# Another order of work in the attention loop of an adaLN, FFT-attention and MoE kernel

## The chip, the cores and the metric

The kernel runs on one core of a Trainium2 chip. The metric is the device time of one execution in microseconds (us), lower is better; the times shown are medians of several executions.

## The reference

Input x is 4 sequences of 1024 tokens with 256 channels, 4096 tokens in all. Cut to what matters:

```python
mod = (silu(c) @ wmod).reshape(4, 6, 1, 256)          # sa, ca, ga, sb, cb, gb; ga, gb kept at least 0.25 from 0
h = layernorm(x) * (1 + ca) + sa
q, k, v = (unit(h @ W.T + b) for each of Wq, Wk, Wv)  # unit(a) = ifft(fft(a) / (|fft(a)| + 1e-8)).real
s = cumsum(bind(k, v), axis=1)                        # bind: product of spectra
x = x + ga * unbind(s, q)                             # unbind: product with the conjugate spectrum
h = layernorm(x) * (1 + cb) + sb
x = x + gb * moe(h)                                   # 8 experts, top 2 of h @ gate_w, swiglu, 256 -> 512 -> 256
```

## The kernel before, in words

The program has three stages: the attention loop (to about 255 us), the routing (to about 300 us) and the expert stage (to the end). The change touches the first and its tail.

The projections and the FFT are one matrix product: `transform_weights` multiplies each of Wk, Wv, Wq with the DFT matrix, so that a projection gives the spectrum at once, with real and imaginary parts of 128 frequencies on the partitions and 512 tokens in a row. The 129th (Nyquist) frequency goes by narrow matmuls of its own (L490, L494). The tokens are worked in 8 blocks of 512 (`NBLK`, t = 0 to 7), two to a sequence. A block passes these steps, engine by engine:

- ScalarE makes the normalized rows (`normal_rows`, L801, with the standard deviation from `project`, L793, and VectorE's `ln1_moments` L1106, L1109 and `ln1_rows` L1117, L1119). TensorE transposes them (L462), ScalarE brings them to SBUF as `h_t` (`spectra`, L815), TensorE multiplies (L484, 24 matmuls, six PSUM banks "z").
- ScalarE evacuates the six banks (`evacuate`, L830), squares them (L840) and the Nyquist columns (L837, L838). VectorE adds the squares (`magnitudes`, L1180), ScalarE takes `roots` (L850).
- VectorE's `bind` (L1132 to L1167) divides by the magnitudes (a reciprocal, L1140), multiplies key and value spectra and sums along the tokens with two scans (L1164, L1167). GpSimd multiplies with the query (L1544, four operations), and on even t scales the inverse DFT for a sequence right behind (L1553, two operations). VectorE's `unbind` (L1174, L1175) adds up, `nyquist_sums`, `nyquist_apply` (L503, L504, L1125) and `nyquist_row` (L560, L946) do the same for the Nyquist row.
- TensorE's `inverse` (L576, L580) goes back to rows of tokens. ScalarE copies them (`residual`, L870), a GpSimd DMA adds x (L1539), VectorE takes moments (`residual`, L1188) and normalizes (`ln2_rows`, L1314, L1319), ScalarE and GpSimd split into two fp16 halves (`split_rows` L881, `low_rows` L1530), TensorE transposes them (`gate_rows`, L515), ScalarE copies (L857), TensorE multiplies by the gate matrix (`gate`, L527), ScalarE copies the gates (L862), and VectorE picks the best two experts (`top2`, L1197, L1201).

Beside this, the expert weights are prepared: SP loads chunks of 512 KB (`load_weights`, L337), ScalarE rounds them to fp16 (`split_weights`, L887), TensorE makes the remainder (`low_piece`, L540, L541; four pieces i = 0 to 3 per block, two chunks), and ScalarE stores it (L894), which frees the stage for the next load.

Every engine has its own queue with a loop written by hand, t from -1 to 7. Iteration t works on several blocks at once: the projection of block t + 1, bind, unbind and inverse of block t, the second normalization of block t - 1, and the gates of block t - 2. The order within an iteration is the order of the calls; the engines meet at semaphores only. The four PSUM banks 4 to 7 go round (`rot`) in an order that `psum_plan` writes out: an item takes the bank of the item four places before it, and TensorE waits (`bank_free`) until that one has been read.

At the start VectorE makes the modulation rows (`modulation`), SP stores them as a small table, broadcasts it and only then loads weight chunks 2 and on. At the end VectorE goes on with `early_picks` for blocks 0 to 5, and the last block runs in halves.

## Time and profile before

| | |
|---|---|
| median of 3 runs | 638.22 us (636.01 to 638.6) |
| the profiled execution, its own time | 634.83 us |
| its span, first to last instruction | 633.0 us |
| mean granted clock of TensorE in it | 0.935 |
| TensorE busy with matmuls | 565.5 us |
| VectorE busy | 490.1 us |
| ScalarE busy | 301.8 us |
| GpSimd busy | 322.2 us |

In the profile PE is TensorE, PEld its weight loads, DVE VectorE, ACT ScalarE, POOL GpSimd and SP SyncE. L484 is line 484 of the kernel. A row of a timeline gives start, duration, engine, line, operation, output from input, how many instructions are merged, and in brackets how long the engine was idle before and what ended the wait. A row of the view by windows gives the window, its length, the busy time of PE, PEld, DVE, ACT and POOL with their instructions, the granted clock of TensorE (1.00 is full), the busy share of the DMA engines and GB/s.

### The profile page before, as it was taken

The page shows a single profiled execution, that of the slowest core. Times are in us where ns is not written, and L with a number is a line of the kernel's source. Part 1 is how long each engine was busy: PE and PEld are TensorE (multiplying, and loading weights), DVE is VectorE, ACT ScalarE, POOL GpSimd, SP SyncE. Part 2 cuts the span into 40 slices and gives each one's busy share as a digit, 9 for nine tenths or more (in the row PEclk, how much of TensorE's full clock was granted, in tenths as well). Part 3 has the DMA queues.
Part 4 walks back from the last instruction along what each step waited for, and adds up shares of the span by engine and source line. Part 5 has one row for each costly group of instructions (what it writes and reads, how often), then busy time and mean ns, then how long its engine had stood idle before and what let it go on. Part 6 is the DMA issues. An engine that isn't in the chain of part 4 may idle for free.

```text
span 633.0 us, 13199 instructions
## 1 busy us (share of the span) xinstructions
PE 565.5 (89%) x4005; PEld 428.1 (68%) x4006; DVE 490.1 (77%) x1058; ACT 301.8 (48%) x497; POOL 322.2 (51%) x213
## 2 busy tenths in 40 slices
PE   6888999899999966559699999999999999999982
PEld 5444554555546543326488888888888888888871
DVE  1238789989998988897378888888888888888881
ACT  3664877877786762532333333333333333333330
POOL 0002132441413243000638888888888888888554
PEclk9798999989997995857799999999999999999996
DMA  9213273652735328622747777777777777777632
GB/s 318 86 61 124 67 204 100 193 149 83 216 101 169 102 88 285 211 38 67 196 62 134 135 138 135 137 136 134 134 135 133 133 133 133 133 134 134 98 35 34
DMA packets 86942, 82.93 MB, mean 131 GB/s; under 512 B 48628, under 2 KB 76276, under 8 KB 86648
## 3 DMA queue, kind: packets, MB, share of 16 engines
q0 software_dynamic: 18480, 34.51, 30.3%
q1 hardware_dynamic: 67128, 47.07, 25.9%
q10 hardware_dynamic: 1296, 0.87, 0.4%
q8 instruction: 21, 0.34, 0.2%
q14 instruction: 17, 0.14, 0.1%
HBM read 45.90 MB, written 23.15 MB: 109 GB/s over the span
## 4 chain that ended last, share of the span: by engine, by line
PE 70%; DVE 12%; ACT 6%; issue 6%; DMA 3%; POOL 1%; POOLq 0%; SPq 0%; ACTq 0%; DVEq 0%
PE ps L703 33%; PE ps L720 16%; PE ps L484 9%; PE ps L540 3%; ACT region L801 2%; PE ps L494 2%; PE ps L636 1%; DMA w_stage<-in_w 1%; ACT region L857 1%; DVE region L1140 1%; DVE region L1180 1%; PE ps L425 1%; POOL region L1544 1%; PE ps L527 1%; DMA region<-in_dft 1%
## 5 line engine op out<-in xcount | busy, mean ns | idle before, releaser
L703 PE MATMUL ps<-region,w_sb 128*128 128x256 f16 x1872 | 213.4, 275 | 2.7 <-ACT region L939 2.7
L703 PEld LDWEIGHTS ps<-region,w_sb 128*128 x1872 | 184.2, 99 | 25.7 <-issue 3.0
L1574 POOL DMA_INDIRECT out_rows<-w_stage,region x78 | 150.5, 1930 | 48.5 <-DVE w_stage L1491 26.5
L1564 POOL DMA_INDIRECT region<-h_scratch,region x78 | 106.0, 1359 | 71.4 <-DVE region L1437 47.9
L1459 DVE TENSOR_SCALAR region<-ps,region 128x256 f32<-128x256 f32 x156 | 68.1, 478 | 61.0 <-PE ps L703 60.9
L720 PE MATMUL ps<-region 128*128 x936 | 110.2, 275 | 3.4 <-DVE region L1473 3.4
L720 PEld LDWEIGHTS ps<-region 128*128 128x128 f16 x936 | 92.3, 99 | 15.0 <-issue 3.6
L1015 ACT ACTIVATE region<-ps,region 128x256 f32<-128x256 f32 x156 | 65.5, 471 | 76.4 <-PE ps L703 76.4
L1025 ACT ACTIVATE region<-region 128x1024 f16<-128x1024 f32 x39 | 41.2, 1058 | 125.3 <-DVE region L1467 125.3
L484 PE MATMUL ps<-region 128*128 128x512 f32 x192 | 88.3, 617 | 8.4 <-ACT region L815 6.0
L1544 POOL TENSOR_TENSOR region<-region 128x512 f32<-128x512 f32 x32 | 39.7, 1267 | 94.3 <-DVE region L1167 94.3
L484 PEld LDWEIGHTS ps<-region 128*128 128x128 f32 x192 | 37.1, 198 | 55.1 <-issue 47.3
L1467 DVE SCALAR_TENSOR_TENSOR region<-region 128x1024 f32<-128x1024 f32 x39 | 47.8, 1225 | 1.4
L1473 DVE SCALAR_TENSOR_TENSOR region<-region 128x1024 f16<-128x1024 f32 x39 | 47.5, 1219 | 1.1 <-ACT region L1025 1.1
L540 PE MATMUL ps<-w_stage,ident_sw 128*128 128x512 f32 x72 | 43.7, 692 | 0.0
L1530 POOL TENSOR_TENSOR region<-region 128x1024 f16<-128x1024 f32 x6 | 12.8, 2129 | 59.7 <-ACT region L881 52.4
L830 ACT ACTIVATE region<-ps,region 128x512 f32<-128x512 f32 x48 | 32.1, 684 | 12.8 <-PE ps L484 12.6
L1491 DVE SCALAR_TENSOR_TENSOR w_stage<-w_stage,region 128x256 f32<-128x256 f32 x78 | 34.0, 477 | 0.0
L1485 DVE SCALAR_TENSOR_TENSOR w_stage<-ps,region 128x256 f32<-128x256 f32 x78 | 29.1, 414 | 4.5 <-PE ps L720 4.5
L894 ACT ACTIVATE w_sb<-ps 128x512 f16<-128x512 f32 x32 | 19.2, 599 | 16.9 <-PE ps L541 16.5
L1140 DVE RECIPROCAL region<-region 128x516 f32<-128x516 f32 x8 | 27.0, 3378 | 0.3
L1464 DVE TENSOR_SCALAR region<-region 128x1024 f32<-128x1024 f32 x39 | 26.6, 683 | 0.0
(208 smaller groups left out, 683.8 us busy)
## 6 DMA issues: line engine op xcount, KB each, us to landing
w_stage<-in_w SPq DMA_DIRECT2D x20, 512.0 KB, 3.6
region<-in_x SPq DMA_DIRECT2D x8, 512.0 KB, 8.2
out_rows<-region SPq DMA_DIRECT2D x8, 512.0 KB, 3.0
h_scratch<-gb_bc SPq DMA_DIRECT2D x4, 1024.0 KB, 6.8
h_scratch<-region SPq DMA_DIRECT2D x8, 512.0 KB, 3.0
region<-region POOLq DMA_DIRECT2D x7, 512.0 KB, 4.6
region<-in_ramp SPq DMA_DIRECT2D x1, 2064.0 KB, 10.8
region<-in_w SPq DMA_DIRECT2D x4, 512.0 KB, 5.1
```

The lines of the kernel that those rows point to most:

```text
L484: mm = pe.matmul(rot(("z", t, i)), w_spec[:, c, k, r * P:(r + 1) * P], h_t[:, k, :], start=(k == 0), stop=(k == KD - 1))
L540: pe.matmul(rot(("lo", t, i)), ident_sw[:], staged(n)[:, at:at + BLK], start=True, stop=False)
L703: mm = pe.matmul(ps[:, GV + 2 * half + a, (f % 2) * MT:(f % 2 + 1) * MT], w, xg_t[:, s, xa * KD + k, :], start=(n == 0), stop=(n == 3 * KD ...
L720: mm = pe.matmul(ps[:, YB + s, u * D:(u + 1) * D], hid[:, s, xa, k, u * P:(u + 1) * P], w, start=(n == 0), stop=(n == 3 * KF - 1))
L1015: ins = nc.scalar.activation(gs[:, 2 * half + f, :], ps[:, 4 + 2 * half, f * MT:(f + 1) * MT], ACT.Gelu_apprx_sigmoid, scale=1.0 / SUP, bi ...
L1025: nc.scalar.activation(hid[:, s, HI], vv[:, s], ACT.Copy, scale=SH / SUP).then_inc(hid_hi, 1)
L1459: ins = V.tensor_scalar(vv[:, s, 2 * half + f, :], ps[:, 5 + 2 * half, f * MT:(f + 1) * MT], b1_t[:, bass.ds(e, 1), 1, 2 * half + f], (LIM ...
L1467: V.scalar_tensor_tensor(out=vv[:, s], in0=vv[:, s], scalar=(1.0 - LIMIT) * SUP, in1=gs, op0=ALU.max, op1=ALU.mult).then_inc(h_ready, 1)
L1473: V.scalar_tensor_tensor(out=hid[:, s, LO], in0=vv[:, s], scalar=SH / SUP, in1=hid[:, s, HI], op0=ALU.mult, op1=ALU.subtract).then_inc(hid ...
L1544: ins = G.tensor_tensor(prod[:, a, r, 0:BLK], s_run[:, s, a, :], z[:, s, QRY, r, 0:BLK], ALU.mult)
L1564: G.indirect_dma_start(out=xg_rows[:, t % XG, u, :], out_offset=None, in_=h_scratch, in_offset=bass.IndirectOffsetOnAxis(ap=gather_idx[:, ...
L1574: G.indirect_dma_start(out=out, out_offset=bass.IndirectOffsetOnAxis(ap=scatter_idx[:, at:at + 1], axis=0), in_=y_sb[:, t % 2, u, :], in_o ...
```

## The change

The work stays the same; its order changes, on all of TensorE, ScalarE and VectorE.

- TensorE: the projection is cut into `project` (transposes), `transform` and `nyquist_cols`. Low piece 0 of a block goes between the last two, low piece 1 ahead of `nyquist_sums`. At t = -1 the transposes of block 1 and low piece 0 come behind the modulation rows. The PSUM plan follows.
- ScalarE: low piece 0 is stored ahead of the third square. The Nyquist columns are copied behind that square, and count `ny_out` twice. Gate rows come ahead of the two standard deviations, these ahead of low piece 1. Normal rows come ahead of low piece 3, and the roots behind it. At the start the roots of block 0 stand between the first two weight splits, the spectra of block 1 follow the modulation copies, and splits 2 and 3 move behind the last bank of block 1.
- VectorE: `top2` works on block t - 3 in place of t - 2 and stands ahead of `nyquist_apply`; `ln1_rows` goes ahead of `unbind`; `modulation` goes into bind(0), behind its second operation, and `magnitudes(0)` no longer waits for it. `top2(5)` comes behind the loop, ahead of `early_picks`.

```diff
--- before.py
+++ after.py
@@
     items = []
     for t in range(-1, NBLK + 2):
         if t + 1 < NBLK:
-            items += [("z", t + 1, i) for i in range(6)] + [("ny", t + 1, 0)]
+            items += [("z", t + 1, i) for i in range(6)]
+        if t == -1:
+            items += [("ny", 0, 0), ("lo", 0, 0)]
+        elif t < NBLK:
+            items.append(("lo", t + 1, 0))
+            if t + 1 < NBLK:
+                items.append(("ny", t + 1, 0))
+        if t < NBLK:
+            items.append(("lo", t + 1, 1))
         if 0 <= t < NBLK:
             items.append(("pre", t, 0))
-        if t < NBLK:
-            items.append(("lo", t + 1, 0))
         if t >= 2:
             items.append(("gate", t - 2, 0))
         if t < NBLK:
-            items += [("lo", t + 1, 1), ("lo", t + 1, 2)]
+            items.append(("lo", t + 1, 2))
         if 0 <= t < NBLK:
             items.append(("row", t, 0))
         if t < NBLK:
@@
             n = place[item] - ROT
             if n >= 0:
                 kind, t, i = order[n]
-                s, v = {"z": (z_ready, 6 * t + i + 1), "ny": (ny_out, t + 1), "pre": (ny_done, t + 1),
+                s, v = {"z": (z_ready, 6 * t + i + 1), "ny": (ny_out, 2 * t + 2), "pre": (ny_done, t + 1),
                         "lo": (w_lo[i % 4 // 2], 2 * t + i % 2 + 1),
                         "gate": (gate_ready, t + 1), "row": (row_ready, t + 1)}[kind]
                 e.wait_ge(s, v)
@@
                 if t >= 4:
                     pe.wait_ge(h2t_ready, KD * (t - 3))
                 transpose_rows(n_sb, t, tp_done)
+
+            def transform(t):
+
                 for i in range(6):
                     c, r = i // 2, i % 2
                     bank_free(pe, ("z", t, i))
@@
                         mm = pe.matmul(rot(("z", t, i)), w_spec[:, c, k, r * P:(r + 1) * P], h_t[:, k, :],
                                        start=(k == 0), stop=(k == KD - 1))
                     mm.then_inc(z_mm, 1)
+
+            def nyquist_cols(t):
+
                 bank_free(pe, ("ny", t, 0))
                 if t == 0:
                     pe.wait_ge(const_in, 48)
@@
 
             transform_weights()
             for t in range(-1, NBLK):
-                if t + 1 < NBLK:
-                    project(t + 1)
                 if t == -1:
+                    project(0)
+                    transform(0)
+                    nyquist_cols(0)
                     modulation_rows()
+                    project(1)
+                    low_piece(0, 0)
+                elif t + 1 < NBLK:
+                    if t >= 1:
+                        project(t + 1)
+                    transform(t + 1)
+                    low_piece(t + 1, 0)
+                    nyquist_cols(t + 1)
+                else:
+                    low_piece(t + 1, 0)
                 if t >= 2:
                     gate_rows(t - 2)
-                if 0 <= t < NBLK:
+                low_piece(t + 1, 1)
+                if t >= 0:
                     nyquist_sums(t)
-                low_piece(t + 1, 0)
                 if t >= 2:
                     gate(t - 2)
-                low_piece(t + 1, 1)
                 low_piece(t + 1, 2)
                 if t >= 0:
                     nyquist_row(t)
@@
                         act.wait_ge(z_mm, 6 * t + 2 * c + r + 1)
                         nc.scalar.activation(z[:, t % 2, c, r, 0:BLK], rot(("z", t, 2 * c + r)), ACT.Identity,
                                              bias=bias_f[:, 3 * r + c:3 * r + c + 1]).then_inc(z_ready, 1)
-                    if c == 2:
-                        act.wait_ge(nymm, t + 1)
-                        if t < 2:
-                            act.wait_ge(ny_zero, t + 1)
-                        cols = rot(("ny", t, 0))[:, 0:3 * TPB].rearrange("p (j c) -> p c j", j=TPB)
-                        nc.scalar.activation(mag[:, t % 2, :, BLK:NB], cols, ACT.Square)
-                        nc.scalar.activation(z[:, t % 2, :, RE, BLK:NB], cols, ACT.Copy).then_inc(ny_out, 1)
+                    if c == 2 and t == 1:
+                        split_weights(2)
+                        split_weights(3)
+                    if c == 2 and t >= 1:
+                        low_piece(t, 0)
                     act.wait_ge(z_ready, 6 * t + 2 * c + 2)
                     nc.scalar.activation(sq[:, c], z[:, t % 2, c, :, 0:BLK], ACT.Square).then_inc(sq_ready, 1)
                     if c == 0 and t >= 2:
                         residual(t - 2)
+                act.wait_ge(nymm, t + 1)
+                if t < 2:
+                    act.wait_ge(ny_zero, t + 1)
+                cols = rot(("ny", t, 0))[:, 0:3 * TPB].rearrange("p (j c) -> p c j", j=TPB)
+                nc.scalar.activation(mag[:, t % 2, :, BLK:NB], cols, ACT.Square).then_inc(ny_out, 1)
+                nc.scalar.activation(z[:, t % 2, :, RE, BLK:NB], cols, ACT.Copy).then_inc(ny_out, 1)
 
             def std2(t):
                 act.wait_ge(ln2_agg, TPB * (t + 1))
@@
 
             def roots(t):
                 act.wait_ge(mag_ready, t + 1)
+                act.wait_ge(ny_out, 2 * t + 2)
                 nc.scalar.activation(mag[:, t % 2], mag[:, t % 2], ACT.Sqrt).then_inc(root_ready, 1)
 
             def gate_rows(t):
@@
                     evacuate(t + 1)
                 if t == LAST:
                     residual(t - 1)
+                    low_piece(NBLK, 0)
+                if t == -1:
+                    split_weights(0)
+                    roots(0)
+                    split_weights(1)
+                    modulation_rows()
+                    spectra(1)
+                    low_piece(0, 0)
                 if t >= 2:
                     gate_rows(t - 2)
-                if t == -1:
-                    split_weights(0)
-                    split_weights(1)
-                    modulation_rows()
-                low_piece(t + 1, 0)
+                if t >= 0 and t + 2 < NBLK:
+                    project(t + 2)
+                if t >= 1:
+                    std2(t - 1)
+                low_piece(t + 1, 1)
                 if t >= 2:
                     gate(t - 2)
-                if t >= 1:
-                    std2(t - 1)
-                if t >= 0 and t + 2 < NBLK:
-                    project(t + 2)
-                low_piece(t + 1, 1)
                 low_piece(t + 1, 2)
                 if t >= 0:
                     nyquist_row(t)
+                if t >= 0 and t + 2 < NBLK:
+                    normal_rows(t + 2)
                 low_piece(t + 1, 3)
-                if t + 1 < NBLK:
+                if 0 <= t < NBLK - 1:
                     roots(t + 1)
                 if t >= 0 and t + 2 < NBLK:
-                    normal_rows(t + 2)
-                if t + 2 < NBLK:
                     spectra(t + 2)
-                if 1 <= t <= NBLK:
+                if t >= 1:
                     split_rows(t - 1)
-                split_weights(2 * t + 4)
-                split_weights(2 * t + 5)
+                if t >= 0:
+                    split_weights(2 * t + 4)
+                    split_weights(2 * t + 5)
 
             last_residual(0)
             last_std(0)
@@
                 dve.wait_ge(eps_ready, t + 1)
                 V.scalar_tensor_tensor(out=den, in0=mag[:, s, KEY, :], scalar=EPS_UNIT, in1=mag[:, s, VAL, :],
                                        op0=ALU.add, op1=ALU.mult).then_inc(den_ready, 1)
+                if t == 0:
+                    modulation()
                 dve.wait_ge(den_ready, t + 1)
                 V.scalar_tensor_tensor(out=rec, in0=mag[:, s, QRY, :], scalar=EPS_UNIT, in1=den,
                                        op0=ALU.add, op1=ALU.mult).then_inc(all_ready, 1)
@@
                     residual(t - 1)
                 if t >= 0 and t + 2 < NBLK:
                     ln1_moments(t + 2)
+                if t >= 3:
+                    top2(t - 3)
                 if 0 <= t < NBLK:
                     nyquist_apply(t)
-                    if t >= 2:
-                        top2(t - 2)
+                    if t + 2 < NBLK:
+                        ln1_rows(t + 2)
                     unbind(t)
                     if t + 1 < NBLK:
                         magnitudes(t + 1)
                 if t == -1:
                     ln1_rows(1)
-                    modulation()
                     magnitudes(0)
-                if t >= 0 and t + 2 < NBLK:
-                    ln1_rows(t + 2)
                 if t >= 1:
                     if t == 1:
                         dve.wait_ge(mod_in, 16)
                     ln2_rows(t - 1)
 
+            top2(LAST - 2)
             early_picks()
             low_rows(LAST - 1)
             for h in range(2):
```

## Rows read from the trace of the kernel before

**Rows 1.** By windows: blocks 2 to 6, expert stage; busy time, clock.

```profile
96.41:232.06 135.65, 127.31 (x630) 75.21 (x630) 124.17 (x271) 102.48 (x156) 44.85 (x36) 0.95 0.47 136
300.00:633.00 333.00, 313.37 (x2827) 277.59 (x2825) 253.93 (x509) 111.80 (x201) 255.88 (x156) 0.97 0.67 123
```

**Rows 2.** What VectorE waited for, 96 to 232 us: total, times, longest.

```profile
DVE best L1197 <- ACT gates L862: 9.4, 5, 2.6
```

**Rows 3.** Timeline of VectorE, block 3 of the loop: start, duration, instruction, idle before.

```profile
122.85 0.42 DVE L1132 TENSOR_SCALAR region<-region 128x516 f32<-128x516 f32 x1
...
135.79 1.26 DVE L1167 TENSOR_TENSOR_SCAN region<-region 128x512 f32<-128x512 f32 x1
...
140.39 0.13 DVE L1125 TENSOR_TENSOR region<-ps,region 128x4 f32<-128x4 f32 x1
142.73 0.37 DVE L1197 MAX8 best<-gates 128x8 f32<-128x8 f32 x4 [2.21 <-ACT gates L862]
...
143.70 0.67 DVE L1174 TENSOR_TENSOR region<-region 128x512 f32<-128x512 f32 x1
...
150.08 0.42 DVE L1132 TENSOR_SCALAR region<-region 128x516 f32<-128x516 f32 x1
```

**Rows 4.** Timeline of VectorE, block 7: last scan and unbind.

```profile
245.01 1.26 DVE L1167 TENSOR_TENSOR_SCAN region<-region 128x512 f32<-128x512 f32 x1
...
251.41 0.69 DVE L1174 TENSOR_TENSOR region<-region 128x512 f32<-128x512 f32 x1 [2.17 <-POOL region L1544]
```

**Rows 5.** Timeline of GpSimd and VectorE where they meet, blocks 0 and 4.

```profile
64.58 1.69 POOL L1553 TENSOR_TENSOR region<-region 128x256 f32<-128x256 f32 x2
...
154.48 2.14 POOL L1530 TENSOR_TENSOR region<-region 128x1024 f16<-128x1024 f32 x1 [12.31 <-ACT region L881]
...
65.69 1.12 DVE L1175 TENSOR_TENSOR region<-region 128x512 f32<-128x512 f32 x1
...
155.41 1.76 DVE L1142 SCALAR_TENSOR_TENSOR region<-region 128x516 f32<-128x516 f32 x1
```

**Rows 6.** Timeline of ScalarE and VectorE at the start of the loop.

```profile
33.25 0.69 ACT L830 ACTIVATE region<-ps,region 128x512 f32<-128x512 f32 x1 [1.03 <-PE ps L484]
...
43.96 1.48 ACT L850 ACTIVATE region<-region 128x1548 f32<-128x1548 f32 x1
...
52.92 1.06 ACT L887 ACTIVATE w_sb<-w_stage 128x1024 f16<-128x1024 f32 x1 [6.13 <-DMA w_stage<-in_w]
...
39.61 0.40 DVE L1092 TENSOR_SCALAR region<-region 4x512 f32<-4x512 f32 x1 [18.67 <-issue]
...
42.11 1.74 DVE L1180 TENSOR_TENSOR region<-region 128x1536 f32<-128x1536 f32 x1
45.48 0.43 DVE L1132 TENSOR_SCALAR region<-region 128x516 f32<-128x516 f32 x1 [1.63 <-ACT region L850]
```

**Rows 7.** Timeline of ScalarE behind unbind, block 3.

```profile
146.24 0.57 ACT L946 ACTIVATE region<-ps 1x512 f32<-1x512 f32 x1
147.26 0.60 ACT L894 ACTIVATE w_sb<-ps 128x512 f16<-128x512 f32 x1 [0.45 <-PE ps L541]
147.75 1.49 ACT L850 ACTIVATE region<-region 128x1548 f32<-128x1548 f32 x1
149.14 2.06 ACT L801 ACTIVATE region<-region 128x256 f32<-128x256 f32 x4
```

**Rows 8.** TensorE, block 3; same work in blocks 3, 5, 6, windows.

```profile
124.57 10.54 PE L484 MATMUL ps<-region 128*128 128x512 f32 x24 [0.53 <-ACT region L815]
...
135.36 1.95 PE L494 MATMUL ps<-region 128*128 128x3 f32 x16
...
137.17:144.47 7.30, 7.30 (x52) 4.56 (x52) 4.99 (x31) 4.19 (x9) 4.96 (x4) 0.53 0.57 181
192.07:199.23 7.16, 7.16 (x51) 4.47 (x50) 4.71 (x31) 4.19 (x9) 4.88 (x4) 0.52 0.66 220
220.22:225.25 5.03, 4.40 (x52) 2.86 (x52) 2.26 (x18) 3.90 (x8) 5.03 (x5) 1.00 0.41 139
```

## The prediction

> **What bounds the kernel now.** I read the stages first (the view by windows), then what VectorE waits for, then one block of the attention loop on each engine, and last the start and the end of the loop. Blocks are counted by t, and a block begins here where VectorE begins bind(t) (L1132).
>
> The five blocks from bind(2) at 96.41 to bind(7) at 232.06 take 135.65 us, 27.13 each. VectorE is busy for 124.17 of them and TensorE for 127.31 [rows 1]. The expert stage from 300 us on is none of the change's lines, with TensorE busy for 313.37 of 333.00; I carry it over unchanged. VectorE's idle time in the five blocks has one cause: top2 waits for the gates that ScalarE copies, 9.4 us in five waits [rows 2]. TensorE is nearly as full, so taking the wait away helps only as far as TensorE, ScalarE and GpSimd keep up.
>
> Block 3 [rows 3]: bind starts at 122.85, its last scan ends at 135.79 + 1.26 = 137.05, so bind is 14.2; the moments go on to 140.39. Top2 can start only at 142.73 and takes 0.97. From unbind's start, 143.70, to bind(4), 150.08, are 6.4: unbind twice 0.6, then magnitudes, ln1_rows (some 0.3) and ln2_rows. In block 7 top2 hardly waits, and what unbind then waits for is GpSimd: the scan ends at 246.27, unbind starts at 251.41, 5.14 later [rows 4]. That is the floor behind the present wait.
>
> **The change, part by part.**
>
> *Top2 a block later, ln1_rows ahead of unbind.* No instruction goes. The gates are then a block old and wait for nothing. Between the scan and unbind VectorE has in block 3 the moments (3.4), nyquist_apply (0.13), top2 (0.97) and ln1_rows (0.3), together 4.8, less than GpSimd's 5.14: the GpSimd floor sets unbind. An odd block becomes 14.2 + 5.14 + 6.4 - 0.3 = 25.4, where 6.4 - 0.3 is 1.2 of unbind and 4.9 behind it.
>
> *Collisions with GpSimd.* In even blocks GpSimd goes on at once with L1553. At t = 0, where unbind too had waited for GpSimd, L1553 starts at 64.58, and unbind's second operation takes 1.12 and ends at 66.81, 2.2 behind that start, against 1.2 in block 3 [rows 3, 5]. Even blocks will meet this each time: I take 2.1. On the other side, at t = 4 the low rows (GpSimd from 154.48) meet L1142, which takes 1.76 [rows 5]. With ScalarE earlier the low rows fall under the reciprocal, so I take 14.0 for an even bind, a little under the 14.2 of block 3; at 14.2 the sum would be 0.6 later. An even block becomes 14.0 + 5.14 + 2.1 + 4.9 = 26.15. The Trainium skill, SBUF — State Buffer, section "SBUF: two separate sides", says that the port pair which VectorE and GpSimd share is an exclusive lock and that the loser blocks for the whole instruction. The trace nearly agrees: the low rows end at 154.48 + 2.14 = 156.62, and L1142, begun at 155.41, ends 0.55 behind that [rows 5]. By the rule in full, with unbind behind both halves of L1553, an even block would by my estimate be up to 0.7 longer, and the forecast some 2.5 us later.
>
> *Five blocks.* Three even and two odd ones: 3 x 26.15 + 2 x 25.4 = 129.3 against 135.65, so 6.35 less, if nothing else comes late.
>
> *ScalarE's order behind unbind.* Today it is nyquist_row 0.57, low piece 0.60, roots 1.49, then normal_rows 2.06 [rows 7]. After: nyquist_row, normal_rows, low piece, roots. As they overlap, 0.6 + 2.0 + 0.5 + 1.5 + 0.1 to see it = 4.7 behind unbind, against VectorE's own 4.9 (magnitudes and ln2_rows). The later roots cost nothing in steady blocks, by 0.2 us only. In block 0 there are no ln2_rows to cover them, and they end 1.3 later than they could; that is in the start below. In exchange normal_rows no longer stand between the roots and the transposes, and TensorE, which waited at that place, goes on straight from inverse.
>
> *Low piece 0 and the Nyquist columns.* TensorE does the same work. ScalarE's third square comes a low-piece copy later, but the magnitudes that need it are several us away. Splitting ny_out costs nothing. Pushing project (ln1's std) ahead of gate and low piece 1 makes these wait for ln1's moments, 3.4 behind the scan; ScalarE leaves the gate rows at about that moment, and behind it wait low piece 1, gate, low piece 2 and the row's bank: 0 to 0.5, hidden, since nyquist_row waits for unbind anyway. The weight loads on SP wait for low piece 3, now some 1.7 later; the load's landing comes shortly ahead of its split, and a late one is covered by ScalarE's slack ahead of the fifth projection bank.
>
> *TensorE's room.* It is busy 25.5 a block, with clock drops in it. In block 3 the granted clock is 0.53 for a stretch right behind the narrow Nyquist matmuls, nearly all of it at the lower level, 1.2 GHz; gate rows to low piece 1 take 7.30 there. In block 5 the same work takes 7.16, and in block 6, at full clock, 4.40 of busy time [rows 8]: 2.9 more for each drop. Without the two, (127.31 - 5.8) / 5 = 24.3, plus 0.5 for the wait for ScalarE's spectra [rows 8], the one that stays: 24.9 against the new 25.8. So it fits, and where a drop comes it does not: of 2.9 I count 1.2 as delay of the next bind (the row then comes 1.4 later, less the 0.2 above). Two drops: 2.4.
>
> *The start.* Today ScalarE evacuates the last bank of block 0 at 33.25 [rows 6], and behind its third square come two weight splits, the modulation copies and low pieces, and the roots only at 43.96, because VectorE makes the modulation rows (39.61 to 42.11) ahead of the magnitudes; bind(0) starts at 45.48 [rows 6]. After: square from 33.9, magnitudes 35.1 to 36.8, roots to 38.3, bind(0) at 38.4. Its first two operations end at 39.6; the modulation waits for ScalarE's copies (roots, one split, then copies: 40.5) and takes 2.6, to 43.1; the rest of bind is 14.0 - 1.2 = 12.8, so the scans end at 55.9, against 45.48 + 14.0 = 59.5. SP waits for the modulation's last operation before it stores the table, broadcasts it and loads weights; that comes 0.9 later. Today ScalarE waits 6.13 for the first of those chunks, to 52.92, ahead of evacuating block 1 [rows 6]; after the change they land at 53.9 and about 55, and ScalarE reaches them at 55.3, behind the last bank of block 1 (TensorE starts that transform at 44.2 behind the low pieces, and it takes 10.5). TensorE then waits for these splits to about 56.4, low piece and Nyquist columns to 59.8, low piece 1 and sums to 61.3; unbind(0) starts at 61.8, ends at 63.7, and nyquist_row to roots takes 4.7: bind(1) at 68.4. Then an odd block, 25.4: bind(2) at 93.9 against 96.41. Gain 2.5, less 0.5 if TensorE's clock drops over its 1.9 us wait (I leave it to the range).
>
> *The end.* Bind(7) on is as today: unbind waits for GpSimd anyway. Top2(4) fills that wait, and top2(5), 0.97, goes ahead of the early picks; VectorE comes to wait for the last residual there, so 0 to 1. Low pieces 0 and 1 leave the path ahead of the last inverse, up to 0.5 gained; if TensorE's clock is low there, up to 1.5 is lost. I take 0.
>
> **Sum.** 2.5 + 6.35 - 2.4 = 6.5 us. The profiled execution took 634.83 (span 633.0), so 628.3 for it. It is 3.4 below the median of the runs shown, 638.22; the same gain from the median is 631.7.
>
> **Rivals.**
> 1. *TensorE sets the pace.* Its order gives it work packed denser, but it is near full, and a clock drop in each block instead of two in five costs three more times 1.2 to 1.5, with something similar in block 1. Gain 2.0: 636.2. For it: 25.5 busy a block. Against: without drops it has 0.9 of room.
> 2. *The roots take the place of the gates.* They have 0.2 us of cover. If ScalarE's row copy is 0.9 later than reckoned, each of seven blocks loses 0.7: 4.9 lost, gain 1.6: 636.6. For it: at 45.48 bind was released by the roots, after 1.63 of waiting [rows 6]. Against: in block 3 the roots end at 149.24, 0.8 before bind(4) [rows 3, 7], and the new order takes 0.6 of it.
> 3. *The slower side: half clock over the projection.* The projection's 24 matmuls take 10.54 at full clock [rows 8]. A stretch of 7 us at half clock, like that of block 3, adds 3.5 there; TensorE's room is 0.9, so 2.6 a block reach VectorE. Three such blocks eat 7.8 and level the gain; all five of the loop give 13, that is 13 - 8.85 = 4.1 slower: 642.3. It decides from the fourth block on. For it: TensorE will stand still ahead of inverse and, in block 0, for the weight splits. Against: the two drops shown came behind the narrow Nyquist matmuls [rows 8], and the change puts full-width work on both sides of them.
> 4. *It does nothing:* the order moves but other waits of the same length come up; 638.
>
> **Chances.** Forecast 0.66; rival 1 0.13, rival 2 0.08, rival 3 0.07, rival 4 0.06. The range runs from 627.0 (no clock drop, 2.4 more, and some on the start and end; 638.22 - 8.85 is 629.4, less the spread of the runs) to 637.0, which takes in rivals 1 and 2. Half a percent, 3.2 us, is what a measurement of this kernel can tell from no change: faster means below 635.0. Faster: most of the forecast and a part of rivals 1 and 2, 0.75; same 0.17; slower 0.08.
>
> **What would show it.** VectorE: no wait at L1197 ahead of the tail; unbind released by GpSimd's multiplications 5.14 behind the scan; even unbinds near 2.1, L1142 at 0.70; blocks of 25.4 and 26.2. bind(0) near 38.4, bind(2) near 93.9, bind(7) near 223 to 226. ScalarE: no 6 us wait for weights at the start. The forecast is wrong if bind waits for roots in many blocks (rival 2), if TensorE's low clock shows in more than half the blocks (rivals 1 and 3), or if the stage from 300 us changes its length.

## The result and the profile after

The changed kernel takes 634.71 us (median of 18 executions, 631.34 to 640.01), the kernel before, on the same chip, 638.64 (18, 636.01 to 641.98). The ratio is 0.9943, 95% interval 0.9920 to 0.9965: faster by 0.57%, 3.9 us between the medians. The forecast was 631.7, a gain of 6.5. The profiled execution took 633.45 (span 631.6) against 634.83 (633.0): only 1.4 us less. That pair alone would mislead, and where the other 5 us of it are is half of what follows. The 634.83 is also none of the 18 executions of before above, and lies below all of them (636.01 to 641.98).

The loop first. The view by windows, with the stretches that answer to [rows 1]:

```profile
95.84:225.29 129.45, 124.97 (x620) 74.15 (x619) 124.89 (x260) 102.11 (x155) 44.86 (x36) 0.95 0.50 143
300.00:631.00 331.00, 314.21 (x2816) 278.00 (x2816) 252.43 (x507) 107.54 (x196) 250.03 (x151) 0.97 0.65 120
```

Five blocks take 129.45 instead of 135.65, and VectorE is busy for 124.89 of them. What it waited for from 96 to 226, 2.4 us in all, which answers to [rows 2]:

```profile
DVE region L1156 <- PE ps L516: 1.5, 1, 1.5
DVE region L1207 <- POOL region L1577: 0.6, 1, 0.6
DVE region L1148 <- ACT region L815: 0.3, 1, 0.3
```

The 9.4 us for the gates are gone. VectorE's timeline, first the end of block 0 with the start of block 1, then block 2 (L1156 is nyquist_apply, L1207 and L1208 unbind, L1163 the start of bind, L1213 the magnitudes):

```profile
53.94 1.20 DVE L1200 TENSOR_TENSOR_SCAN region<-region 128x512 f32<-128x512 f32 x1
...
63.16 0.16 DVE L1156 TENSOR_TENSOR region<-ps,region 128x4 f32<-128x4 f32 x1 [6.30 <-PE ps L516]
...
63.52 0.69 DVE L1207 TENSOR_TENSOR region<-region 128x512 f32<-128x512 f32 x1
...
64.72 1.75 DVE L1213 TENSOR_TENSOR region<-region 128x1536 f32<-128x1536 f32 x1
70.34 0.43 DVE L1163 TENSOR_SCALAR region<-region 128x516 f32<-128x516 f32 x1 [3.87 <-ACT region L877]
...
115.02 1.12 DVE L1207 TENSOR_TENSOR region<-region 128x512 f32<-128x512 f32 x1
116.06 1.12 DVE L1208 TENSOR_TENSOR region<-region 128x512 f32<-128x512 f32 x1
...
122.01 0.42 DVE L1163 TENSOR_SCALAR region<-region 128x516 f32<-128x516 f32 x1
```

Block 0 loses: 6.30 for TensorE's sums, then 3.87 for the roots. What held them, on TensorE (L552, L553 a low piece, L506 the Nyquist columns, L515 and L516 the sums) and ScalarE (L823 normal_rows, L921 a low piece's copy, L877 the roots):

```profile
55.81 1.12 PE L552 MATMUL ps<-w_stage,ident_sw 128*128 128x512 f32 x2 [1.72 <-ACT w_sb L914]
...
57.40 2.73 PE L506 MATMUL ps<-region 128*128 128x3 f32 x16
59.99 2.05 PE L552 MATMUL ps<-w_stage,ident_sw 128*128 128x512 f32 x2
61.84 0.63 PE L553 MATMUL ps<-w_sb,ident_neg 128*128 128x512 f16 x1
...
62.55 0.57 PE L516 MATMUL ps<-region 128*128 128x4 f32 x2
```

TensorE's window there (columns as in [rows 1]; the granted clock is the third number from the end):

```profile
60.00:63.00 3.00, 3.00 (x9) 1.69 (x9) 0.00 (x0) 0.93 (x4) 1.44 (x3) 0.50 0.00 0
```

```profile
66.39 2.06 ACT L823 ACTIVATE region<-region 128x256 f32<-128x256 f32 x4
68.36 0.57 ACT L921 ACTIVATE w_sb<-ps 128x512 f16<-128x512 f32 x1
68.84 1.48 ACT L877 ACTIVATE region<-region 128x1548 f32<-128x1548 f32 x1
```

TensorE waits 1.72 for the weight splits, and within the Nyquist columns, which take 2.73 where [rows 8] has 1.95, its clock falls to the lower level (0.50): the next low piece takes 2.05 + 0.63 where one at full clock takes 1.02 + 0.38. So bind(2) starts at 95.84, only 0.57 earlier than in [rows 1], though bind(0) started at 37.90, 7.58 earlier than in [rows 6]. From there the loop gains to 6.77 at bind(7), and all of it lasts to the first gather (292.55 against 299.32). The rest of the loss is at the entry of the expert stage, on TensorE (L705 transposes a tile's rows, L725 is the up-projection):

```profile
299.91 7.34 PE L725 MATMUL ps<-region,w_sb 128*128 128x256 f16 x47 [1.30 <-ACT region L966]
...
309.63 0.55 PE L705 MATMUL ps<-ident_h,region 128*128 128x128 f16 x7 [1.19 <-issue]
312.05 8.19 PE L725 MATMUL ps<-region,w_sb 128*128 128x256 f16 x48 [1.87 <-ACT region L966]
...
322.70 5.40 PE L725 MATMUL ps<-region,w_sb 128*128 128x256 f16 x48
```

and in the chain of waits that ended last (start, length, what):

```profile
303.72 6.12 another core or an unknown queue
```

From the first up-projection to the third are 22.79 us; in the profile of before they were 17.75:

```profile
306.19 8.03 PE L703 MATMUL ps<-region,w_sb 128*128 128x256 f16 x48 [1.30 <-ACT region L939]
...
323.94 5.40 PE L703 MATMUL ps<-region,w_sb 128*128 128x256 f16 x48
```

Of the 6.77 us gained at the first gather 5.04 go there. Is that the change's doing?

### The profile page after: what moved, and what is told of

Read it like the earlier page. It is cut to its first block, busy times and chain, and to the rows that moved or that the text cites. A ratio compares the mean times of both kernels' runs of the same rounds, so it can differ in the third digit from the quotient of the medians.

```text
span 631.6 us, 13207 instructions
## 1 busy us (share of the span) xinstructions
PE 570.7 (90%) x4005; PEld 431.1 (68%) x4006; DVE 492.5 (78%) x1058; ACT 301.1 (48%) x497; POOL 321.2 (51%) x213
## 4 chain that ended last, share of the span: by engine, by line
PE 64%; DVE 25%; issue 5%; ACT 3%; POOL 1%; another core or an unknown queue 1%; DMA 1%; POOLq 0%; ACTq 0%; DVEq 0%
PE ps L725 32%; PE ps L742 16%; PE ps L493 5%; DVE region L1173 3%; PE ps L552 2%; DVE region L1137 2%; DVE region L1213 2%; DVE region L1352 2%; PE ps L648 1%; DVE region L1347 1%; DVE region L1188 1%; DVE region L1182 1%; DVE region L1197 1%; DVE region L1200 1%; PE ps L506 1%
## 5 line engine op out<-in xcount | busy, mean ns | idle before, releaser
L725 PE MATMUL ps<-region,w_sb 128*128 128x256 f16 x1872 | 215.7, 276 | 3.4 <-ACT region L966 3.2
L725 PEld LDWEIGHTS ps<-region,w_sb 128*128 x1872 | 185.4, 99 | 27.2 <-issue 3.6
L493 PE MATMUL ps<-region 128*128 128x512 f32 x192 | 86.2, 606 | 3.9 <-ACT region L837 3.9
L552 PE MATMUL ps<-w_stage,ident_sw 128*128 128x512 f32 x72 | 46.9, 739 | 2.9 <-ACT w_sb L914 1.7
L921 ACT ACTIVATE w_sb<-ps 128x512 f16<-128x512 f32 x32 | 18.8, 588 | 15.8 <-PE ps L553 15.5
## 6 DMA issues: line engine op xcount, KB each, us to landing
region<-in_ramp SPq DMA_DIRECT2D x1, 2064.0 KB, 11.3
```

Source lines behind the costliest of these rows:

```text
L493: mm = pe.matmul(rot(("z", t, i)), w_spec[:, c, k, r * P:(r + 1) * P], h_t[:, k, :], start=(k == 0), stop=(k == KD - 1))
L552: pe.matmul(rot(("lo", t, i)), ident_sw[:], staged(n)[:, at:at + BLK], start=True, stop=False)
L725: mm = pe.matmul(ps[:, GV + 2 * half + a, (f % 2) * MT:(f % 2 + 1) * MT], w, xg_t[:, s, xa * KD + k, :], start=(n == 0), stop=(n == 3 * KD ...
```

## Experiments

Twelve runs in four groups, each group on one chip: top2 alone, the loop's part, the start's part and block 0 eased; the changed kernel again, roots first and block 0 in the old order; before again and the loop's part again; the last three. Each ratio is to executions of the kernel before on that chip, whose medians in the four groups are 634.01, 639.37, 638.58 and 634.33, so the chips differ by up to 5.4 us, as much as the change is worth. Profiled moments are compared with [rows 1] and [rows 6].

**Top2 alone.** Before, with top2 moved and nothing else.

```diff
+                if t >= 3:
+                    top2(t - 3)
                 if 0 <= t < NBLK:
                     nyquist_apply(t)
-                    if t >= 2:
-                        top2(t - 2)
                     unbind(t)
...
+            top2(LAST - 2)
             early_picks()
```

> The kernel before with one part of the change: top2 one block later and ahead of nyquist_apply. Theory A (the wait for the gates was the whole of the loop's loss; the new orders on ScalarE and TensorE only keep it away): VectorE's wait for the gates goes, unbind is released by GpSimd in each block, bind(2) to bind(7) takes 129 to 131 us instead of 135.65, and the run is 5 to 6.5 us ahead at the first gather, 0.5 to 0.9% less in the time. Theory B (the order of ScalarE matters as much: with the gates still behind the std and the square roots, everything that ScalarE does behind them comes late and the roots or nyquist_row take the place of the gates): bind(2) to bind(7) takes 132 to 134 us and the gain is 2 to 3.5 us.

632.55 us against 634.01, ratio 0.9985 (0.9955 to 1.0016): nothing. The wait for the gates is gone, as theory A said, and the time has not changed: bind(7) starts at 232.04, where it was at 232.06. Odd blocks fell from 27.2 or 27.4 to 26.4, even ones rose from 27.5 or 27.1 to 28.3 and 28.0. Block 4 on VectorE (L1142 is a step of bind, L1174 unbind), then GpSimd (L1531, the low rows):

```profile
149.28 0.43 DVE L1132 TENSOR_SCALAR region<-region 128x516 f32<-128x516 f32 x1 [0.59 <-ACT region L850]
...
154.62 2.56 DVE L1142 SCALAR_TENSOR_TENSOR region<-region 128x516 f32<-128x516 f32 x1
...
170.32 1.11 DVE L1174 TENSOR_TENSOR region<-region 128x512 f32<-128x512 f32 x1 [0.74 <-POOL region L1545]
171.36 1.12 DVE L1175 TENSOR_TENSOR region<-region 128x512 f32<-128x512 f32 x1
```

```profile
154.49 2.13 POOL L1531 TENSOR_TENSOR region<-region 128x1024 f16<-128x1024 f32 x1 [12.30 <-ACT region L881]
```

The low rows start at 154.49; in [rows 5] they started at 154.48. ScalarE releases them, and its pace had not changed. VectorE, 0.8 us earlier, now meets them whole: L1142 takes 2.56 instead of 1.76 there and 0.70 where they don't meet. Unbind, earlier too, runs into L1553's pair. Followed through: unbind(3) starts at 142.22 instead of 143.70, 1.48 earlier. The roots, at the same time as before because ScalarE waits for TensorE's low pieces (1.59 at L894), take 0.59 of it at bind(4) (and 0.57 at bind(6)), the low rows take 0.80, and unbind(4) ends where it did. Theory B named ScalarE and the roots, and part of the loss is there; the larger part, the low rows, neither theory had.

**The loop's part alone.** The changed kernel with the old start: modulation ahead of magnitudes(0) again, and on ScalarE

```diff
                     split_weights(0)
-                    roots(0)
                     split_weights(1)
                     modulation_rows()
-                    spectra(1)
                     low_piece(0, 0)
...
-                if 0 <= t < NBLK - 1:
+                if t < NBLK - 1:
                     roots(t + 1)
```

> The changed kernel with the start as it was before: no modulation inside bind(0), roots(0), spectra(1), the splits and the projection of block 1 in the old places. Theory A (the start is worth next to nothing, as its gain is eaten by nyquist_apply(0) waiting for TensorE): bind(0) near 45.5, bind(2) within 1 us of 96.4, bind(2) to bind(7) 129.5 us, time within 0.15% of the changed kernel. Theory B (the start is worth 2 to 3 us, and only the profiled run hid it): 0.3 to 0.5% slower than the changed kernel.

628.52 us (6 executions), ratio 0.9901 (0.9869 to 0.9933); but the profiled one was the slowest (633.02), with bind(0) at 47.94 and bind(2) at 99.84, so it was run again. The theories compared it with the changed kernel, which is not in this group; its median and those of the start's part and of block 0 eased (628.85, 628.15, below) agree within the intervals.

> The loop's new order with the old start, once more, since the profiled execution of the first run was its slowest (633.0 against 626.8 to 629.6) and had TensorE's clock at 0.90 in the first 100 us. Theory A (the loop's part is 6 to 7 us): bind(0) near 45.5, bind(2) within 1 us of 96.4, bind(7) near 226; 0.9 to 1.1% faster than before, no worse than the changed kernel (0.9943 and 0.9930 of before). Theory B (the loop loses in blocks 0 and 1 what it gains later): bind(2) near 99 again, bind(7) near 230, 0.3 to 0.6% faster.

637.85 us against 638.58, ratio 0.9982 (0.9950 to 1.0013), on another chip. No single number fits this kernel. Its twelve executions go with TensorE's mean granted clock: 632.8 to 633.0 at 0.94, one 635.1 at 0.93, 637.8 to 638.3 at 0.924 or 0.925, 640.5 to 641.2 at 0.915; those of before in that group lie between 636.0 and 641.9 at 0.927 to 0.933. The profiled one, at 0.924, has blocks 3, 4 and 5 at 26.59, 27.47 and 26.03, where the changed kernel has 25.47, 26.16 and 25.48, and block 0 at 28.34. In block 4 TensorE's window (columns as in [rows 1]), its low piece, and VectorE's next bind:

```profile
166.00:172.00 6.00, 6.00 (x55) 4.32 (x55) 5.54 (x32) 3.59 (x9) 5.78 (x6) 0.62 0.86 258
```

```profile
167.55 2.02 PE L552 MATMUL ps<-w_stage,ident_sw 128*128 128x512 f32 x2
...
178.80 1.04 PE L468 MATMUL ps<-ident_sb,region 128*128 128x128 f32 x8
```

```profile
178.90 0.43 DVE L1155 TENSOR_SCALAR region<-region 128x516 f32<-128x516 f32 x1 [1.07 <-ACT region L872]
```

So the half clock that costs the changed kernel's profile nothing costs this one 1.3 in block 4. The profile is theory B's (bind(2) at 98.68, bind(7) at 231.09), the time below even that. Block 0, in the new order with the old start, is longer in both profiles of this kernel (26.42 and 28.34) than before (25.13). Theory A's 0.9 to 1.1% shows only in the first run; that the clock makes the difference is read from the times and this one profile, no run shows it by itself.

**The start's part alone.** Before, with roots(0), spectra(1), the transposes of block 1 and the modulation where the change puts them, and the splits 2 and 3 one square later than there; TensorE's and ScalarE's order from block 0 on as before.

```diff
                     split_weights(0)
+                    roots(0)
                     split_weights(1)
                     modulation_rows()
+                    spectra(1)
...
+                if t == 0:
+                    modulation()
                 dve.wait_ge(den_ready, t + 1)
```

> The kernel before with the start of the change alone. Theory A: bind(0) near 38, but nyquist_apply(0) waits some 6 us for TensorE's sums, so that bind(2) is at most 1 us earlier than 96.41, and the loop from there takes 135.7 us as before: 0 to 0.15% faster. Theory B (without the loop's new order in block 0, where the roots stand ahead of normal_rows, bind(1) comes 2 us earlier than in the changed kernel, and the start keeps its 2.5 us): bind(2) near 94, 0.3 to 0.4% faster.

628.85 us, ratio 0.9935 (0.9907 to 0.9964). Bind(1) starts at 67.01 and bind(2) at 92.78, 3.6 ahead of before: theory B, and more than it said. The blocks from bind(2) to bind(7) take 133.26 here, 2.4 less than before, which no theory had. TensorE waits for the splits here too, 1.78, and runs at the lower clock after it, but the sums of block 0 stand ahead of that wait (L506, L507), so unbind is released by GpSimd and only the roots are still waited for, 1.27:

```profile
56.08 0.36 PE L507 MATMUL ps<-region 128*128 128x4 f32 x2
58.22 2.07 PE L543 MATMUL ps<-w_stage,ident_sw 128*128 128x512 f32 x2 [1.78 <-ACT w_sb L896]
```

```profile
61.62 1.11 DVE L1188 TENSOR_TENSOR region<-region 128x512 f32<-128x512 f32 x1 [3.39 <-POOL region L1557]
...
67.01 0.43 DVE L1144 TENSOR_SCALAR region<-region 128x516 f32<-128x516 f32 x1 [1.27 <-ACT region L859]
```

**Block 0 eased.** The changed kernel with nyquist_sums(0) right behind transform(1), and roots(1) ahead of nyquist_row(0); the two are not told apart.

```diff
                     transform(t + 1)
+                    if t == 0:
+                        nyquist_sums(0)
                     low_piece(t + 1, 0)
...
                 low_piece(t + 1, 2)
+                if t == 0:
+                    roots(1)
                 if t >= 0:
                     nyquist_row(t)
```

> The changed kernel with block 0 eased: TensorE makes the Nyquist sums of block 0 between the transform of block 1 and low piece 0, so ahead of the weight splits it waits for, and ScalarE makes the roots of block 1 ahead of nyquist_row and normal_rows. Theory A (the start's predicted 2 us were lost to these two orders): nyquist_apply(0) no longer waits over 1 us for TensorE, unbind(0) starts near 61 instead of 63.5, bind(1) near 66 instead of 70.3, bind(2) near 92, the first gather 3 to 4 us earlier, 0.4 to 0.6% faster than the changed kernel. Theory B (TensorE's own work in blocks 0 and 1 sets the pace there, so what is gained at bind(1) is lost at the projection of block 2): bind(1) earlier by 3 us, but bind(2) by under 1, and no difference in the time.

628.15 us, ratio 0.9908 (0.9876 to 0.9941). Unbind(0) at 61.62 and bind(1) at 67.23, 3.1 earlier than in the changed kernel; bind(2) at 95.62, 0.2 earlier: theory B by these moments. The time can't be set beside the changed kernel's, which is not in this group. The new order puts two low pieces ahead of the sums in block 1 as well, and TensorE, which starts the next transform 5.2 us behind bind(1) (3.6 with the start alone) and falls to half clock again, ends them late:

```profile
88.71 0.16 DVE L1162 TENSOR_TENSOR region<-ps,region 128x4 f32<-128x4 f32 x1 [1.23 <-PE ps L518]
```

**The changed kernel again.**

> The changed kernel, not altered. It tells whether the loss at the entry of the expert stage (first gather 6.8 us earlier than before, but the third up-projection only 1.2 us earlier) belongs to the change or to one execution. Theory A (one execution's clock and stall): the second up-projection again near 309 to 310 us, as the first gather is at 292.5, and a span near 627 us if nothing else comes. Theory B (the change's shorter routing window brings the stall): second up-projection near 312, span 630 to 632 us again.

633.16 us against 639.37, ratio 0.9930 (0.9903 to 0.9956). The entry stall came back unchanged: first up-projection at 299.73, second at 311.71, third at 322.44. That seemed theory B, until before was profiled again (below).

**Roots first.** The changed kernel with one piece undone.

```diff
-                if t >= 0 and t + 2 < NBLK:
-                    normal_rows(t + 2)
                 low_piece(t + 1, 3)
                 if 0 <= t < NBLK - 1:
                     roots(t + 1)
+                if t >= 0 and t + 2 < NBLK:
+                    normal_rows(t + 2)
```

> The changed kernel with one piece undone: ScalarE makes the square roots of block t+1 ahead of normal_rows(t+2), as before. Theory A (normal_rows early is what keeps GpSimd's low rows under VectorE's reciprocal): in blocks 2, 4 and 6 the low rows start 3.3 to 5.2 us behind bind instead of 2.3 to 2.8, and where it is over 4, L1175 takes 1.7 to 2.6 us instead of 0.69 and the block 27 to 28.3 instead of 26.17; bind(2) to bind(7) takes 131 to 134 us; block 0 on the other hand becomes 2 us shorter, as bind(1) no longer waits for the roots. Together -2 to +2 us against the changed kernel. Theory B (the place of normal_rows does not matter with the gate copies ahead of the std): every block stays at 26.2 and 25.5, and the kernel is 2 us faster than the changed one through block 0 alone.

637.87 us, ratio 0.9978 (0.9959 to 0.9996), 4.7 us above the changed kernel of the same group. Theory A, with a bigger loss: bind(2) to bind(7) takes 134.74. The low rows start 3.6 us behind bind in blocks 2 and 3, 4.05 in 4 and 6, and 5.21 in 5; L1175 takes 0.98, 1.41 and 2.55 where the changed kernel has 0.69. Over the five blocks that is 3.9 of the 5.3 us lost (134.74 against 129.45); the rest goes with waits for TensorE's sums (3.8 us in four, against 1.5 in one). Block 5, VectorE then GpSimd:

```profile
180.71 2.55 DVE L1175 SCALAR_TENSOR_TENSOR region<-region 128x516 f32<-128x516 f32 x1
```

```profile
180.58 2.13 POOL L1563 TENSOR_TENSOR region<-region 128x1024 f16<-128x1024 f32 x1 [11.22 <-ACT region L908]
```

In the changed kernel the low rows start 2.27 to 2.82 behind bind and end inside the reciprocal, which takes the 3.38 it takes everywhere. Block 4, VectorE then GpSimd:

```profile
149.39 3.38 DVE L1173 RECIPROCAL region<-region 128x516 f32<-128x516 f32 x1
```

```profile
150.30 2.13 POOL L1563 TENSOR_TENSOR region<-region 128x1024 f16<-128x1024 f32 x1 [8.97 <-ACT region L908]
```

Seven of the fourteen profiles (before in both, top2 alone, the start alone in both, block 0 eased, this one) have the step behind the reciprocal lengthened by the low rows. It ends 0.54 to 0.56 us behind them each time, however early it had begun. Block 0 became 1.4 us shorter, not 2.

**Block 0 in the old order.** The changed kernel, but for t = 0 TensorE's and ScalarE's order of before, with the splits kept early and the bank plan to match.

```diff
+                elif t == 0:
+                    transform(1)
+                    nyquist_cols(1)
+                    nyquist_sums(0)
+                    low_piece(1, 0)
                 elif t + 1 < NBLK:
...
                     roots(t + 1)
+                if t == 0:
+                    normal_rows(2)
```

> The changed kernel with block 0 in the old order on TensorE (Nyquist columns and sums of block 0 ahead of low piece 0) and ScalarE (roots ahead of normal_rows), and the weight splits ahead of the last square; from block 1 on the new order. Theory A (the change's start and its loop are each worth their gain, but the new order costs 3 us in block 0): bind(0) near 38.5, TensorE waits under 1 us for the splits, bind(1) at 66.5 to 67.5, bind(2) at 92.5 to 93.5, bind(7) near 222 to 223, some 3 us earlier than the changed kernel and 9 to 10 earlier than before; time 1.2 to 1.5% below before. Theory B (TensorE is behind from block 0 on and its low pieces stand in block 1's way): bind(2) near 95.5 as in the run with block 0 eased, no gain over the changed kernel.

629.34 us, ratio 0.9872 (0.9845 to 0.9900), on the chip where the changed kernel had 0.9930. Theory A: bind(1) at 64.74, bind(2) at 90.23, bind(7) at 220.76, 11.3 earlier than before. The splits are ready when TensorE comes to them, and there is no wait and no clock drop (from the second run of this kernel, below):

```profile
55.39 0.36 PE L518 MATMUL ps<-region 128*128 128x4 f32 x2
55.61 1.10 PE L554 MATMUL ps<-w_stage,ident_sw 128*128 128x512 f32 x2
```

**Before again.**

> The kernel before, not altered, for a second profile of it. Its first profile has no stall at the entry of the expert stage: from the first up-projection at 306.19 to the second 9.9 us, where four runs of the new order (the changed kernel twice, roots first, block 0 in the old order) have 12.0 to 12.1. Theory A (the stall belongs to a chip or an execution, not to the order of the loop): this profile can show it too, second up-projection 12 us behind the first, with ScalarE and VectorE standing until the same moment; the span is then 636 to 637 us instead of 633. Theory B (the change brings it): 9.9 us again. A profile without the stall at a time of 635 or less tells only that the fast case was met again.

638.88 against 638.58, ratio 0.9997 (0.9975 to 1.0020). The profile (span 637.6) has the stall. TensorE, then ScalarE and VectorE, which both stand until 317.2:

```profile
307.16 7.85 PE L703 MATMUL ps<-region,w_sb 128*128 128x256 f16 x48 [1.30 <-ACT region L939]
...
316.93 0.27 PE L683 MATMUL ps<-ident_h,region 128*128 128x128 f16 x2 [1.15 <-issue]
319.27 6.93 PE L703 MATMUL ps<-region,w_sb 128*128 128x256 f16 x48 [2.07 <-ACT region L939]
...
328.66 5.40 PE L703 MATMUL ps<-region,w_sb 128*128 128x256 f16 x48
```

```profile
317.18 0.84 ACT L1015 ACTIVATE region<-ps,region 128x256 f32<-128x256 f32 x2 [6.21 <-remote]
```

```profile
317.17 1.66 DVE L1459 TENSOR_SCALAR region<-ps,region 128x256 f32<-128x256 f32 x4 [11.56 <-remote]
```

Theory A: the stall comes without the change too. The third up-projection comes at 328.66, 21.50 behind the first.

**The three on one chip.**

> The start's part alone, on one chip with the two runs that follow, since the parts have so far been timed on different chips. Theory A (each part is worth its gain, and the change loses some of the start's in block 0): bind(1) near 67, bind(7) near 226 to 227, 0.5 to 0.8% below before, the same as the changed kernel within the intervals. Theory B (the 0.65% of the first run was that chip's): 0 to 0.3% below before.

> The new order with block 0 in the old order, again. Theory A: bind(7) near 221, 1.1 to 1.4% below before, 3 to 5 us below both the start alone and the changed kernel. Theory B (the loop's new order gives its gain back to TensorE's clock drops wherever those come, as in the second run of the loop alone): no more than 2 us below the start alone.

> The changed kernel on the same chip: 0.4 to 0.8% below before by both theories; by theory A 3 to 5 us above the run before this one.

Before 634.33 us. The start alone 630.11, ratio 0.9952 (0.9922 to 0.9983); block 0 in the old order 624.58, 0.9859 (0.9822 to 0.9897); the changed kernel 628.94, 0.9943 (0.9909 to 0.9976). The version with block 0 in the old order beats both kernels in both its groups, here by 4.4 us the changed one and by 9.8 the one before: all three times are theory A's, or 0.1% beside it. The moments of the start alone are not. Its profiled execution was one of its two slowest (635.34, clock 0.927), with bind(1) at 70.92 and bind(7) at 232.41 where its first profile had 67.01 and 226.04. Of these last 6.4 us 3.9 are there at bind(2) already, and the five blocks take 135.70. In block 0 TensorE runs longer at the lower clock behind its wait for the splits (two groups at 2.07 and 1.92; the first profile had 2.07, then 1.46), ScalarE copies those pieces ahead of the roots, and bind(1) waits for the roots:

```profile
70.92 0.43 DVE L1144 TENSOR_SCALAR region<-region 128x516 f32<-128x516 f32 x1 [3.86 <-ACT region L859]
```

So sums ahead of the wait keep unbind(0) safe, but not the roots. The changed kernel's third profile has no stall:

```profile
298.27 7.08 PE L725 MATMUL ps<-region,w_sb 128*128 128x256 f16 x48 [1.30 <-ACT region L966]
...
307.19 5.41 PE L725 MATMUL ps<-region,w_sb 128*128 128x256 f16 x48 [1.40 <-ACT region L966]
...
315.06 5.40 PE L725 MATMUL ps<-region,w_sb 128*128 128x256 f16 x48
```

16.79 from the first to the third. Its span is 624.2, 8.8 below the first profile of before (633.0), which has no stall either.

## Why the prediction was right, and where it was not

Right in sign, and 634.71 lies in the range of 627.0 to 637.0. The forecast of 631.7 was 3 us too low: a gain of 3.9 for a predicted 6.5, and 6.2 and 5.4 in the two groups that repeated it. That the profiled pair stands 6.77 apart at the first gather, close to the 6.5, is partly luck: the start gave 1.9 less than its term, and the clock drops took none of the 2.4 set down for them.

*Five blocks, 6.35 less:* held. 129.3 predicted, 129.45, 129.49 and 129.44 in three profiles; even blocks 26.17 for 26.15, odd ones 25.48 for 25.4. The GpSimd floor is the right one (unbind 5.15 behind the scan), and even unbinds take 1.12 + 1.12, close to the 2.1 taken from [rows 5]. The 0.7 that by the prediction's estimate the rule of exclusive ports in the Trainium skill (SBUF — State Buffer, "SBUF: two separate sides") would have added to even blocks did not come. On the larger overlap the trace does agree with it: L1142 or L1175 always ends 0.55 behind the low rows.

*"With ScalarE earlier the low rows fall under the reciprocal":* held, and it was worth more than the prediction saw. I priced it as 0.2 of an even bind. Top2 alone gains nothing, and undoing normal_rows' place alone costs 5.3 us over five blocks (134.74 against 129.45). The prediction credited the gain to the removed wait for the gates. The runs show that the removal alone is taken back by the roots and the low rows, and that with it normal_rows' place on ScalarE is needed to keep the gain. The other new orders of the loop (gate rows, standard deviations, low piece 0) were not tried one by one.

*Two clock drops, 2.4:* right neither in number nor in price. In the profiled execution three stretches at half clock in the five blocks, near 136, 188 and 214 us, delayed no bind. With blocks 0, 1 and 7 the lower clock shows in six of eight blocks, which the prediction had named as a sign against itself; the sign came, the cost did not, outside block 0. Over executions time goes with the clock: the changed kernel's third run took 626.0 to 628.6 at 0.934 or more, and 628.9 to 633.6 at 0.928 or less. That would be rival 1 (TensorE sets the pace) in the slower ones, but none of the three profiles of the changed kernel is of one of them, so where the slower ones lose is not shown.

*The start, 2.5:* the step that failed. Bind(0) came at 37.90 for 38.4 and the scans ended at 55.1 for 55.9, but of the 2.5 only 0.57 was left at bind(2) (0.75 and 1.8 in the other two profiles). The prediction had "low piece 1 and sums to 61.3"; they ended at 63.12. I had seen TensorE's wait for the splits (1.9 for a measured 1.72) and left a clock drop behind it to the range as 0.5; it was 1.8, with the sums standing behind a whole low piece at half clock. Block 0 in the old order, with no wait and no drop there, has bind(1) at 64.74 and 64.70. The start alone, with the sums ahead and the drop behind them, has it at 67.01 and 70.92.

*The end, 0:* held; from bind(7) to the first gather it is 67.26 in both.

*The expert stage, carried over unchanged:* wrong for the profiled pair; a change of this stage's length was another sign that the prediction had named against itself. The profile that I reckoned from was stall-free, and at 634.83 it was 3.4 below its median and below the fastest of the 18. I took note of the first and asked no further. It fits the chips of the first and fourth group, where before has 634.01 and 634.33; on which chip it was taken is not on record here. The stall goes with 21.50 - 17.75 = 3.75 in before and 22.79 - 16.79 = 6.0 in the changed kernel. Part of either is the up-projection behind it, which then ran in part at the lower clock (6.93 and 8.19 against 5.41). Pairs of the same kind differ more than the recorded pair: 6.2 with the stall (spans 637.6 and 631.4) and 8.8 without it, though on different chips. Whether the change makes the stall longer stays open: from the first to the third up-projection are 21.50 in before, 21.93 in the loop's part with the old start, and 22.66 to 22.79 in the four profiles with the new start and loop.

*Rivals 2 and 3* are not seen in the changed kernel's profile: bind waits for the roots at bind(0) and bind(1) alone (1.56 and 3.87), the projection's 24 matmuls of blocks 1 to 7 take 10.46 to 10.54, and no clock drop delayed a bind of the five blocks. Rival 2's wait is real elsewhere: 0.96 at bind(6) in block 0 in the old order, 1.03 and 1.07 at bind(4) and bind(5) in the loop's part again.

*Slips in the working:* 24.3 + 0.5 is 24.8, not 24.9, and the drop in block 5 cost 7.16 - 4.40 = 2.8, not 2.9; nothing hangs on either. The gates were also not the one cause of VectorE's idle time: 135.65 - 124.17 is 11.5, of which they are 9.4.

## What to carry to other kernels

A wait on the bounding engine is not yet a gain: look at what the engines behind it do at the moment that the wait would end, and whether their work (here GpSimd's low rows, fixed by ScalarE) then falls on an instruction that it collides with. Moving work ahead of a product that another engine waits for is safe only while the mover is ahead (with the same start bind(1) comes at 70.34 in the new order of block 0 and at 64.74 in the old); at the start of a pipeline, where it still waits for its inputs, keep the old order. And when a profiled execution lies some us off its median, a second profile of the same kernel comes before any comparison by it.

## What had not been expected of the hardware

At the entry of the expert stage TensorE, ScalarE and VectorE stand together until nearly one moment (309.63, 309.96 and 309.96 in the changed kernel's first profile; 316.93, 317.18 and 317.17 in before's second), with the releaser given as "remote" and TensorE's as "issue". In the loop's part again the three moments lie further apart (314.02, 315.67, 315.81). It shows in six of the fourteen profiles: the first of the changed kernel, and all five of the second and third group, with both orders of the loop among them. It shows in none of the seven of the first and fourth group, which ran on other chips, nor in the first of before. The kernel before tells the same chips apart: its median is 638.58 to 639.37 where the stall shows, and 634.01 and 634.33 where it does not. The profiles with it are 3.75 to 6 us longer there. What releases it, and whether the chip decides it, stays open: nothing in the trace answers to it, and no run was made to find it.

The same kernel's executions on one chip differ by over 8 us, and go with the mean granted clock (632.8 at 0.94, 641.2 at 0.915, in the second run of the loop's part). Which way the cause runs, no run here shows.
